# A graph layer with scattered edge sums: opening in another order, and table rows of 68 words

## The reference, cut to what matters

```
xn = layernorm(x)                                  # 3125 nodes, 256 wide
sums = segment_sum(edge_attr_64, src, 3125)        # 53125 edges, 64 wide
counts = segment_sum(ones, src, 3125)
agg = sums / maximum(counts, 1)
gnn = relu(concat([xn, agg, u[0]]) @ W1 + b1) @ W2 + b2
mix: q, k, v = xn @ Wqkv.T + b, per head of 32, q and k normalized
     kv_mod = sum_n kn_i kn_j v1_e / N             # pairs of key elements
     y = 0.5 qn qn kv_mod + s^2 qn kv + s^4 vsum;  y = y[1:] / y[0];  y @ Wproj.T + b
x = x + gnn + mix
x = x + moe(layernorm(x))                          # 8 experts, the best 2 each
```

## Time and profile before

| what | value |
|---|---|
| median of three runs | 1052.55 us |
| the profiled execution | 1047.74 us, span 1046.0 us |
| busy, share of the span | PE 81%, POOL 68%, DVE 60%, ACT 40% |
| mean granted clock of TensorE | 0.897 of full speed |
| moved by DMA | 117.36 MB |

### The profile page before, as it was taken

The page is one execution under the profiler, slowest core; times in us unless marked ns, Lnnn a source line. Parts: engine busy times, 40 slices in busy tenths (PEclk is TensorE's granted clock), DMA queues, the critical chain, the costliest instruction groups (busy, mean ns, idle before and its releaser), DMA issues.

```text
span 1046.0 us, 19213 instructions
## 1 busy us (share of the span) xinstructions
PE 846.4 (81%) x6172; PEld 518.1 (50%) x6172; DVE 626.9 (60%) x2123; ACT 416.5 (40%) x1087; POOL 709.5 (68%) x511
## 2 busy tenths in 40 slices
PE   2597796997999999999999999991099980899940
PEld 1243343444444545545455555551088870899940
DVE  3599997997575354454654646550367774555535
ACT  2444544333454344344443434430045550566630
POOL 4768877588878878888888888888230567645430
PEclk7689988898999999999999999996589985899985
DMA  9736565255655455565565555433972524344449
GB/s 311 151 60 108 83 128 82 35 83 104 123 102 97 57 90 93 82 114 83 93 112 87 95 93 105 50 38 22 217 247 59 153 95 130 108 131 125 131 129 279
DMA packets 146342, 117.36 MB, mean 112 GB/s; under 512 B 109023, under 2 KB 132131, under 8 KB 145606
## 3 DMA queue, kind: packets, MB, share of 16 engines
q1 hardware_dynamic: 81156, 73.77, 25.0%
q0 software_dynamic: 58080, 27.96, 24.0%
q10 hardware_dynamic: 7010, 14.42, 4.3%
HBM read 73.12 MB, written 44.07 MB: 112 GB/s over the span
## 4 chain that ended last, share of the span: by engine, by line
PE 50%; DVE 19%; POOL 13%; issue 7%; DMA 6%; ACT 3%; ACTq 0%; SPq 0%; POOLq 0%; DVEq 0%
POOL edge_sums L690 12%; DVE r2t L1640 9%; PE ps L1311 7%; PE ps L1121 5%; PE ps L1522 5%; PE ps L1533 5%; PE ps L1298 3%; PE ps L1247 3%; PE ps L1261 3%; PE ps L1451 3%; DMA r2t<-expert_outputs 2%; DVE same L1577 2%; PE ps L1189 2%; PE ps L1168 2%; POOL routed_rows L709 2%
## 5 line engine op out<-in xcount | busy, mean ns | idle before, releaser
L690 POOL DMA_INDIRECT edge_sums<-sums,addr x368 | 575.6, 1564 | 156.4 <-issue 129.6
L1677 DVE TENSOR_SCALAR oh<-node,dsrc 128x500 bf16<-128x500 int16 (+1 forms) x336 | 100.1, 358 | 52.3 <-PE ps L1311 51.7
L914 ACT ACTIVATE r<-ps 128x500 f32<-128x500 f32 (+1 forms) x224 | 103.4, 548 | 69.8 <-PE ps L1247 69.7
L1577 DVE SCALAR_TENSOR_TENSOR same<-srow,src_f,below 128x128 f32<-128x128 int32 x368 | 105.8, 344 | 21.1 <-DMA srow<-in_src_row 15.6
L1311 PE MATMUL ps<-oh,r2t 128*64 128x500 bf16 (+1 forms) x1008 | 117.2, 366 | 1.4 <-DVE oh L1677 1.3
L1121 PE MATMUL ps<-edges,same 128*128 128x65 f32 x736 | 102.2, 284 | 18.9 <-issue 12.2
L1121 PEld LDWEIGHTS ps<-edges,same 128*128 128x128 f32 x736 | 92.5, 197 | 42.7 <-issue 29.5
L1640 DVE TENSOR_TENSOR r2t<-ps,r 125x4096 f32<-125x4096 f32 x25 | 110.3, 4413 | 0.0
L1168 PE MATMUL ps<-r2t,r 125*32 125x512 f32 x400 | 64.3, 772 | 46.5 <-DVE r2t L1640 46.4
L721 POOL DMA_INDIRECT expert_outputs<-r x56 | 54.5, 974 | 55.9 <-DVE r L2030 49.5
L1311 PEld LDWEIGHTS ps<-oh,r2t 128*64 128x64 bf16 x1008 | 50.5, 112 | 66.2 <-issue 39.9
(11 more groups left out here) (284 smaller groups left out, 1372.2 us busy)
## 6 DMA issues: line engine op xcount, KB each, us to landing
srow<-in_src_row SPq DMA_DIRECT2D x46, 512.0 KB
edges<-in_edge_attr SPq DMA_DIRECT2D x23, 512.0 KB, 4.8
r<-routed_rows SPq DMA_DIRECT2D x56, 129.0 KB, 2.1
r<-hpre_rows SPq DMA_DIRECT2D x12, 500.0 KB
edge_sums<-sums,addr POOLq DMA_INDIRECT x368, 3.2
edge_sums<-r SPq DMA_DIRECT2D x4, 1040.0 KB, 13.2
r2t<-in_ew SPq DMA_DIRECT2D x4, 1024.0 KB, 10.0
hpre_rows<-r ACTq DMA_DIRECT2D x16, 250.0 KB, 2.4
```

Source lines behind the costliest of these rows:

```text
L690: pool.indirect_dma_start(out=tables[k], out_offset=bass.IndirectOffsetOnAxis(ap=addr[:, j:j + 1], axis=0), in_=sums[:, j % OR, :], in_off ...
L914: act.activation(phT[:, R % 2, h, 0:n], bank(BP[h], 128, 0, n), ACT.Square).then_inc(pair_squares, 1)
L1577: v.scalar_tensor_tensor(same[:, j % SR, :], srow[:, c % 2, j % RH * 128:(j % RH + 1) * 128], src_f[:, j:j + 1], below[:, :], ALU.is_equal ...
L1677: v.tensor_scalar(oh[:, (2 * i + a) % OHS, 0:nt * P].rearrange("p (t n) -> p t n", t=nt), node16[:, 0:nt, :], dsrc[:, 2 * w + a:2 * w + a ...
```

## The change

`TW` becomes 68, so that the rows of the four tables, the slots of `sums` and the zeroed stretch shrink from 80 to 68 words. `PRE` becomes 6: six groups are released ahead of the first tile, tile t releases group 6 + t, and 60 groups are left to the 54 rounds. In the opening, PE does `dedup` of groups 0 and 1 first and that of groups 2 to 5 behind the first projections; ACT copies groups 2 and 3 behind `x_sums(1)`, groups 4 and 5 behind `x_squares(1)`. DVE takes `x_scales(0)` right behind the bias, then builds `pick2` and the small constants, then compares groups 2 to 5, and groups 6 and 7 in tile 0. In the first pass `x_scales` stands behind `k_pairs` and `k_unit` of its tile.

```diff
--- before.py
+++ after.py
@@ -28,11 +28,11 @@
     DCH = ND // DW
     G4 = 4
     NGR = ETS // G4
-    TW = 80
+    TW = 68
     TROWS = 3328
     SR = 16
     OR = 28
-    PRE = 4
+    PRE = 6
     XC = 5
     HID = W1.shape[1]
     MC = HID // 128
@@ -852,8 +852,6 @@
                 sums_copy(g)
             x_sums(0)
             x_squares(0)
-            for g in range(2, PRE):
-                sums_copy(g)
             for k in range(G4):
                 act.wait_ge(tables_zeroed[k], 16)
             xn_of(0)
@@ -869,7 +867,11 @@
             xn_of(3)
             xT_copy(2)
             x_sums(1)
+            for g in range(2, 4):
+                sums_copy(g)
             x_squares(1)
+            for g in range(4, PRE):
+                sums_copy(g)
 
             for t in range(T):
                 k_squares(t)
@@ -1125,7 +1127,7 @@
             pe.wait_ge(consts, 21)
             for b in (BS,) + BM:
                 mm(bank(b), lhsT=zeros[:, 0:128], rhs=zeros[:, 0:1].to_broadcast([128, BANK]), start=True, stop=False, skip_group_check=True)
-            for g in range(PRE):
+            for g in range(2):
                 dedup(g)
             pe.wait_ge(pick_ready, 1)
             for c in range(QC):
@@ -1208,6 +1210,8 @@
             keys_values(0)
             keys_values(1)
             xT_of(2)
+            for g in range(2, PRE):
+                dedup(g)
             pe.wait_ge(consts, 23)
             for t in range(T):
                 pair_moments(t)
@@ -1593,9 +1597,14 @@
             link(v.tensor_tensor(brest[:, :], brest[:, :], bparts[:, 1, :], ALU.subtract))
             v.tensor_copy(bparts[:, 2, :], brest[:, :]).then_inc(bias_ready, 1)
 
-            for g in range(2, PRE):
-                compare(g)
-
+            def x_scales(c):
+
+                v.wait_ge(std_ready, c + 1)
+                here = slice(c * XC, (c + 1) * XC)
+                link(v.reciprocal(rstd[:, here], rstd[:, here]))
+                v.tensor_tensor(x_shift[:, here], neg_mean[:, here], rstd[:, here], ALU.mult).then_inc(rstd_ready, 1)
+
+            x_scales(0)
             v.wait_ge(consts, 21)
             link(v.tensor_reduce(unit2[:, 0:D], ident[:, :].rearrange("p (b d) -> p d b", b=4), AX.X, ALU.add))
             link(v.tensor_copy(unit2[:, D:2 * D], unit2[:, 0:D]))
@@ -1603,18 +1612,10 @@
                             unit2[:, 0:D].unsqueeze(1).unsqueeze(1).to_broadcast([128, 1, OFF, D]),
                             turned(unit2[:, :], 1, 1, 2 * D), ALU.add).then_inc(pick_ready, 1)
 
-            def x_scales(c):
-
-                v.wait_ge(std_ready, c + 1)
-                here = slice(c * XC, (c + 1) * XC)
-                link(v.reciprocal(rstd[:, here], rstd[:, here]))
-                v.tensor_tensor(x_shift[:, here], neg_mean[:, here], rstd[:, here], ALU.mult).then_inc(rstd_ready, 1)
-
-            x_scales(0)
             link(v.tensor_reduce(head4[:, :], ident[:, :].rearrange("p (h d) -> p h d", h=4), AX.X, ALU.add))
             v.tensor_copy(block[:, :, :], head4[:, :].unsqueeze(2).to_broadcast([128, 4, D]))
             link(v.tensor_tensor(fold[:, :], ident[:, 0:EA], ident[:, EA:128], ALU.add))
-            for g in (PRE, PRE + 1):
+            for g in range(2, 6):
                 compare(g)
 
             def heads(ap, w):
@@ -1680,10 +1681,13 @@
             v.wait_ge(bias_spread, 48)
             k_norm(0)
             for t in range(T):
+                k_pairs(t)
+                k_unit(t)
                 if t % XC == 0 and t + 5 < T:
                     x_scales((t + 5) // XC)
-                k_pairs(t)
-                k_unit(t)
+                if t == 0:
+                    for g in range(6, PRE + 2):
+                        compare(g)
                 k_norm(t + 1)
                 for g in pass1_groups(t):
                     compare(g + 2)
```

## The result

The changed kernel takes 1022.68 us, the median of 4 runs (1017.23 to 1026.43); the kernel before 1052.57 beside it. The ratio is 0.9745, with a 95% interval of 0.9702 to 0.9788: 26.8 us faster, between 22 and 31. The prediction was 1028.0, a gain of 24.5, and lies inside its range. The profiled execution took 1024.87 us, its span is 1023.1.

A forecast was written before the change was run, and what follows sets the result against it. POOL's scatters, 7.48 us a group behind the last starved group, bound the kernel; S 13.0 + 1.2 + 7.5 gives 21.9 us at the last scatter, plus 2.6 in the tail: 24.5 off 1052.55, so 1028.0, range 1020 to 1040.

The forecast's parts named there:

- the other limit: POOL running without a gap from group 2's start at 37.7: last scatter at 710.5, a gain of 26.5 us.
- S: Lead of the other engines at the first pass's end, from moving the scales: 13.0 us, ends 0 and 18.4.
- The opening: Part of the lead won by the second k_pairs, starting at 46.0 instead of 52.91: 6.9 us, taken as 7.0.
- The later tiles: At tiles 5, 10 and 15, three DVE waits of 2 us for ACT's statistics vanish behind the product: 6.0 us.
- The late sums of group 2: In the opening, group 2's sums wait on ACT for x_sums(1); its scatter starts at 37.7, 4.4 us later.
- One group of the two: Two extra groups in hand: one left behind the last starvation, worth 7.5 us; the other saved by round 27, 1.2 us.
- The tail: Reading back the tables behind the last scatter shrinks with rows of 68 words: 2.6 us, bounds 0 and 3.3.
- The later tiles keep their time: Rival, 20%: the three waits of 2 us only move to k_norm; lead 7.0, gain 18.5 us, 1034 us.
- POOL never starves: Rival, 12%: the first pass's lead is over 17.8 us; gain 29 to 30 us, 1023 us.
- The lead is given back: Rival, 10%: PE replaces DVE as the first pass's bound, lead about 0; gain 10 us, 1042.5 us.
- Scatters land late: Rival, 5%: 272-byte rows make scatters land late; gain gone from a landing of 7.5, at 8.3 the kernel takes 1123 us.
- k_pairs at 33 and 46: Sign in the opening that the forecast is right: the first two pair products on DVE start at 33 and 46 us.

The follow-up runs named there:

- scales0_behind: The changed kernel with the scales of the first tiles behind the comparisons of groups 2 and 3 again: 1026.43 us, ratio 0.9778.
- scales_ahead_late: The changed kernel with the scales ahead of the product again in tiles 5, 10 and 15, not in tile 0: 1030.37 us, ratio 0.9826.
- scales_ahead: The changed kernel with the scales ahead of the product again in tiles 0, 5, 10 and 15: 1033.97 us, ratio 0.9855.
- rounds50: The changed kernel with the 60 groups of the second pass spread over 50 rounds instead of 54: 1020.81 us, ratio 0.9721.
- rows68_alone: The kernel before with rows of 68 words instead of 80 and nothing else: 1048.23 us, ratio 0.9974.
- six_in_old_order: The kernel before with six groups instead of four ahead of the first tile, old order of the opening kept: 1047.14 us, ratio 0.9972.
- rounds50_group2: rounds50 with the sums of group 2 and the copies of groups 2 and 3 moved earlier: 1017.05 us, ratio 0.9683.
- scales_behind_alone: The kernel before with only the scales moved behind the product in tiles 0, 5, 10 and 15: 1037.62 us, ratio 0.9877.
- four_groups: The changed kernel with four groups instead of six ahead of the first tile, new order kept: 1032.09 us, ratio 0.9836.

## Why the prediction was right

**The bound and the formula.** The prediction said that the last scatter is set by the last starved group and the 7.48 us pace behind it. It gave group 62 at 491.1 and the end at 715.1; measured are 492.05 and 716.56. From 492.05 to the start of group 91 at 709.44 are 29 groups of 7.50. The kernels with one part taken away bear it out: a lead lost comes back at the last scatter with its size, as it stands in scales0_behind (4.1 and 4.1 us), and within 0.5 us in scales_ahead_late and scales_ahead once the handover between the passes is allowed for. With no starvation left (rounds50) the other limit, group 2's start, sets it within 1 us. That the gain comes so close to the forecast in the profiles is in part luck, as the next paragraph shows.

**S, the lead of the first pass.** Predicted 13.0, measured 240.6 - 226.3 = 14.4 at tile 24. Several deviations nearly cancel. The opening gave 5.3 us, not 7.0. The first product came at 35.9 instead of 33.5, since the rows of group 4 landed at 32.0, where I had them 1.6 us before the old 31.15. The second, on which the 5.3 rests, came 1.6 us late because ACT's second statistics were ready at 42.2 and not at 40.6 (DVE waited 1.61 us for them). The later tiles gave more than 6.0: 10.1 between tiles 1 and 16, of which 7.1 lie at tiles 5, 10 and 15; 1.0 was lost again up to tile 24. Behind the first pass 13.3 us are left at round 27 where S + 1.2 should have been 15.6. The prediction took it that both kernels run alike there, and in these two executions they didn't: 4.0 us were lost in the handover at the low clock, and 1.7 won back since only the kernel before had the drop of the clock at 332 us. The drop at 332 us doesn't belong to the change, as rows68_alone and six_in_old_order have the old scales and no such drop; whether the long handover does is open.

**The late sums of group 2.** Predicted 37.7, measured 39.77, 6.25 us of idle POOL. In the changed kernel it is hidden, since groups 61 and 62 starve behind it; rounds50_group2 shows that it is the next thing to pay for once the starvation at round 27 is gone.

**One group of the two.** The 7.5 us are borne out by six_in_old_order, which ends 0.4 us earlier with a lead of -10.0: with the clock allowed for, the two groups give 8.6 us in all. The split into 7.5 and 1.2 was not measured by itself.

**The tail.** Predicted 2.6, measured 3.5 in the pair of profiles and 2.4 over all of them. By an estimate from the 358 GB/s of the Trainium skill (DMA: Bandwidth & Descriptors, Specifications) it would have been 1.7; the spread of the tails is too large to tell these apart.

**The rivals.** "The later tiles keep their time" falls with scales_ahead_late and scales_behind_alone. "POOL never starves" fails in the trace, where groups 61 and 62 starve and POOL ends 4.0 us later than without a gap; its 1023 lies nearer to the median of 1022.68 than the forecast of 1028.0 does, but not by its mechanism (see "The size"). "The lead is given back" falls: 14.4 us of lead are there at tile 24, and PE's wait for the products is still 31.4 us. "Scatters land late" falls with rows68_alone; no run here shows how rows split into pieces, only that either length lands alike. The forecast row "k_pairs at 33 and 46" was off by 2.9 and 1.6 us.

**The size.** The predicted 24.5 us stand against 26.8 (22 to 31) by the runs and 22.9 by the spans. The sum was made for the profiled execution: 1023.2, measured 1024.87. The step from there to a median failed: 4.8 us were added, since the profiled execution before lay 4.8 under its median, while the profiled one after lies 2.2 over its own. Two of the four executions took 1017 and 1020 us at a granted clock of 0.912 and 0.913, the two others 1025 and 1026 at 0.904 and 0.903. Of the parts, the scales behind the product are worth 12 us alone, the rows 2 to 3. The groups in hand give 9.6 us by the ratios in the new order and 2.9 in the old; the new order without them gives some 2 to 3, the 5.5 us of the medians (4.3 by the ratios) from scales_behind_alone to four_groups less the rows.

## What to carry to other kernels

Where one engine works through a fixed number of equal pieces, write its end as (start of the last starved piece) + (pieces left) x (pace), and ask of each edit which of these it moves; a reserve of pieces helps only up to the place where the reserve was planned to be used up. A wait that stands ahead of work which doesn't need it can be moved behind it, and two lines moved gave nearly half of the gain here. When the starved engine is the bound, a schedule for the others that releases early can cost nothing, as in rounds50, even where it fills the ring and makes them wait. Before two profiles are compared to a few us, compare a stretch in which both do the same work: here one such stretch alone differed by 4 us.

## What the runs showed that was not expected

The versions differ in how much their runs spread. The kernel before spans 1044.0 to 1054.4 in 23 runs and four_groups 1027.1 to 1036.0 in six, while rounds50 spans 1019.1 to 1022.2 and rounds50_group2 1015.6 to 1018.8, five each. In the last two POOL has no gap; in the first two the last starved group waits for PE's rounds, and a TensorE with a granted clock of 0.897 to 0.909 (four_groups) then moves the end. The profiles show one part of it: the handover between the passes took 17.4 to 17.7 us in seven of them and 21.5 to 21.8 in five, at mean granted clocks of 0.80 to 0.81 and 0.60 to 0.61. In rounds50 the long form cost nothing, as POOL had groups in hand. That this is the cause of the whole spread is argued, not shown.

The opening itself varies from execution to execution. PE's first group waits for the first edges, and started at 12.18 us in the kernel before and at 14.72 in the changed kernel, with the first copies and statistics behind it; but in rounds50, whose opening is the changed kernel's, it started at 11.22, the comparison of group 4 at 30.06 instead of 32.02, and the first product at 33.9 instead of 35.9. The prediction's 33.5 was thus within what the same code does, and its miss of 2.4 us says little on its own.
